# Scores by pairs of heads, with the last product of wide tiles in two 64-row halves

## The reference

```
q_nop = (c_Q @ Wq_up)          # 16 heads x 128
q_pe  = rope(c_Q @ Wq_pe)      # 16 heads x 64
k_nop, v = split(c_KV @ Wkv_up)  # 8 heads x 128 each, each used by two query heads
k_pe  = rope(rms_norm(x @ Wk_pe))  # 64, shared by all heads
scores = ([q_nop, q_pe] . [k_nop, k_pe]) * 192**-0.5, causal mask
y = softmax(scores) @ v
out = y @ Wo
```

## Time and profile before

| | us |
|---|---|
| median of 3 timed runs (lowest, highest) | 1826.86 (1822.85, 1830.7) |
| profiled execution, its own time | 1830.16 |
| its span, first to last instruction | 1828.4 |
| TensorE busy | 1724.3 (94%) |
| VectorE busy | 1293.5 (71%) |
| ScalarE busy | 1129.1 (62%) |
| GpSimd busy | 423.1 (23%) |
| mean granted TensorE clock (share of full) | 0.984 |

### The profile page before, as it was taken

How to read it: one execution, slowest core, us unless ns; L and a number is a source line. 1 busy time by engine, 2 the same in 40 slices (tenths; PEclk the granted TensorE clock), 3 DMA queues, 4 the chain that set the end, 5 groups by cost and what they waited for, 6 DMA issues and landing times.

```text
span 1828.4 us, 29329 instructions
## 1 busy us (share of the span) xinstructions
PE 1724.3 (94%) x9200; PEld 903.2 (49%) x9200; DVE 1293.5 (71%) x3368; ACT 1129.1 (62%) x2463; POOL 423.1 (23%) x1042
## 2 busy tenths in 40 slices
PE   4678999999999999999999999998999999999998
PEld 3344455544454545545554445554445444555443
DVE  5667677768677677776767777776767767777674
ACT  5566666657566566655656566665656656666563
POOL 1223222122221222222221222212222222221110
PEclk9799999999999999999999999999999999999999
DMA  9336788877868888785978867787876878877775
GB/s 257 82 63 113 129 138 156 153 134 139 144 115 158 149 145 147 144 150 92 161 127 158 154 124 139 146 149 129 146 143 127 152 138 147 150 144 145 144 147 104
DMA packets 911733, 255.05 MB, mean 139 GB/s; under 512 B 897368, under 2 KB 899674, under 8 KB 911194
## 3 DMA queue, kind: packets, MB, share of 16 engines
q1 hardware_dynamic: 902336, 235.29, 72.9%
q10 hardware_dynamic: 8794, 15.80, 2.8%
q0 software_dynamic: 448, 2.10, 0.5%
HBM read 20.32 MB, written 8.39 MB: 16 GB/s over the span
## 4 chain that ended last, share of the span: by engine, by line
PE 63%; issue 12%; DVE 10%; DMA 8%; ACT 3%; POOL 3%; SPq 1%; DVEq 0%; ACTq 0%; POOLq 0%
DMA FT<-F 6%; PE bank L539 5%; PE bank L543 5%; PE bank L542 5%; PE bank L540 5%; PE bank L541 5%; PE bank L563 5%; PE bank L564 4%; PE bank L565 4%; PE bank L580 4%; PE bank L582 4%; PE bank L581 4%; DVE F L1244 2%; DVE P L1230 2%; DMA Q<-QS 1%
## 5 line engine op out<-in xcount | busy, mean ns | idle before, releaser
L838 ACT ACTIVATE P<-P,nm 128x512 f32<-128x512 f32 (+7 forms) x512 | 395.5, 772 | 614.7 <-DVE nm L1230 613.6
L1230 DVE CUSTOM_DVE_ANT_0 P<-bank,mask,neg 128x512 f32<-128x512 f32 (+7 forms) x512 | 416.5, 814 | 330.9 <-PE bank L543 326.5
L1244 DVE SCALAR_TENSOR_TENSOR F<-P,rc,F 128x512 f16<-128x512 f32 (+7 forms) x512 | 420.1, 821 | 4.5 <-ACT F L833 3.8
L833 ACT ACTIVATE F<-P,rc 128x512 f16<-128x512 f32 (+7 forms) x512 | 389.7, 761 | 19.0 <-DVE rc L1238 12.7
L1417 POOL TENSOR_SCALAR sn<-sm 128x1 f32<-128x1 f32 x512 | 140.6, 275 | 578.0 <-ACT P L838 575.3
L539 PE MATMUL bank<-K,Q 128*128 128x512 f16 (+3 forms) x768 | 251.3, 327 | 5.4 <-DMA Q<-QS 5.1
L563 PE MATMUL bank<-FT,V 128*128 128x512 f16 x576 | 220.3, 382 | 34.9 <-DMA FT<-F 33.0
L541 PE MATMUL bank<-K,Q 128*128 128x512 f16 (+3 forms) x768 | 251.3, 327 | 0.0
L542 PE MATMUL bank<-K,Q 128*128 128x512 f16 (+3 forms) x768 | 251.3, 327 | 0.0
L540 PE MATMUL bank<-K,Q 128*128 128x512 f16 (+3 forms) x768 | 251.3, 327 | 0.0
L543 PE MATMUL bank<-K,Q 128*128 128x512 f16 (+3 forms) x768 | 251.2, 327 | 0.0
(11 more groups left out here) (191 smaller groups left out, 2596.6 us busy)
## 6 DMA issues: line engine op xcount, KB each, us to landing
out<-X ACTq DMA_DIRECT2D x32, 256.0 KB, 3.7
X<-in_x ACTq DMA_DIRECT2D x28, 256.0 KB, 3.1
FT<-F SPq DMA_TRANSPOSE x352, 4.2
wo<-in_Wo SPq DMA_DIRECT2D x4, 1024.0 KB, 9.3
V<-CC SPq DMA_DIRECT2D x32, 64.0 KB, 2.0
Q<-QS SPq DMA_TRANSPOSE x128, 4.1
X<-in_x SPq DMA_DIRECT2D x4, 256.0 KB, 7.5
ua<-in_Wq_up SPq DMA_DIRECT2D x1, 1024.0 KB, 9.3
```

The source lines that it names most:

```text
L833: return e.eng.activation(dst, src, ACT.Copy, scale=scale)
L838: e.eng.activation(m.P[:, u % 4, 0:w], m.P[:, u % 4, 0:w], ACT.Exp, bias=m.nm[:, u % 8:u % 8 + 1], scale=-1.0, accum_out=m.sm[:, u % 8:u % ...
L1230: e.eng.tensor_tensor_reduce(out=m.P[:, u % 4, 0:w], in0=m.pS[u % 2][:, off:off + w], in1=m.mask[:, 1024 - w:1024], scale=m.neg[:, :], sca ...
L1244: e.eng.scalar_tensor_tensor(out=m.F[:, slot, at + w:at + 2 * w], in0=m.P[:, u % 4, 0:w], scalar=m.rc[:, u % 8:u % 8 + 1], in1=m.F[:, slot ...
```

## The change

TensorE's score goes by pairs of heads (`pair(n, p)`, heads 2p and 2p+1), at quarters 0 and 2. In tiles with i >= 4 (`halved`) the first four products of both heads come first; then the last product is done with 64 rows for each head: for the even head rows 0 to 63 of block 8+h and of BLO, for the odd head rows 64 to 127, into the two heads' different banks, cut by cut. For this the rotated query parts lie as high, low, low, high in a pair of heads (`rotated_parts`), so that both heads' high part is where its half reads it; the product of low with low is no longer made in these tiles. `combine` is done in two halves, after quarters 1 and 3. The lists of VectorE, ScalarE, GpSimd and SyncE go by pairs too: two maxima one after the other, two exponents, both scaled parts, two transposes.

```diff
+def halved(i):
+    return i >= 4
...
+def rotated_parts(m, n):
+    return m.QS[:, n % 2, 1024:1536].rearrange("p (h a d) -> p h a d", h=2, a=4)
...
+    def pair(n, p):
...
+        for h in (2 * p, 2 * p + 1):
+            u = 4 * n + h
+            e.wait_ge(s.mk, u - 1)
+            for lo, hi in cuts:
+                o, keys = m.pS[u % 2][:, off + lo:off + hi], slice(base + lo, base + hi)
+                e.eng.matmul(o, Q[:, h, :], K[:, AHI, keys], start=True, stop=False)
+                e.eng.matmul(o, Q[:, h, :], K[:, ALO, keys], start=False, stop=False)
+                e.eng.matmul(o, Q[:, 4 + h, :], K[:, AHI, keys], start=False, stop=False)
+                e.eng.matmul(o, Q[:, 8 + h, :], K[:, BHI, keys], start=False, stop=False)
+                if not halved(i):
+                    op = e.eng.matmul(o, Q[:, 8 + h, :], K[:, BLO, keys], start=False, stop=True)
+            if not halved(i):
+                op.then_inc(s.s, 1)
+        if halved(i):
+            for lo, hi in cuts:
+                for h, top in ((2 * p, 0), (2 * p + 1, 64)):
+                    o, keys = m.pS[h % 2][:, off + lo:off + hi], slice(base + lo, base + hi)
+                    op = e.eng.matmul(o, Q[top:top + 64, 8 + h, :], K[top:top + 64, BLO, keys], start=False, stop=True)
+                    if hi == cuts[-1][1]:
+                        op.then_inc(s.s, 1)
...
-            if n + AHEAD < N:
-                score(n + AHEAD, q)
+            if q % 2 == 0 and n + AHEAD < N:
+                pair(n + AHEAD, q // 2)
...
-            if q == 3 and n:
-                combine(n - 1)
-    combine(N - 1)
+            if q % 2 and n:
+                combine(n - 1, q // 2)
+    combine(N - 1, 0)
+    combine(N - 1, 1)
```

VectorE's list of a block, after the change (ScalarE's, GpSimd's and SyncE's are changed alike):

```diff
+        wide = n + AHEAD < N and halved(where(n + AHEAD)[1])
+        for p in range(2):
+            u = 4 * (n + AHEAD) + 2 * p
+            if p == 0 and t and g == 1:
+                accumulate(t - 1)
+            if p == 0 and n and wide:
+                values_lo(n - 1)
             if u < 4 * N:
                 maximum(u)
+                maximum(u + 1)
+            if p == 0 and n and not wide:
+                values_lo(n - 1)
...
             if u <= 4 * N:
                 scaled_lo(u - 2)
+            if p == 0 and n + 2 * AHEAD < N:
+                queries.rotate(n + 2 * AHEAD)
+            if u <= 4 * N:
+                scaled_lo(u - 1)
+            if u < 4 * N:
+                inverse(u)
+                inverse(u + 1)
+            if p and n + 2 * AHEAD < N:
                 queries.queries_lo(n + 2 * AHEAD)
...
+            if t + LEAD < T and (g, p) == (2, 0):
+                tiles.x_signs(t + LEAD)
```

More of the change, by code:

```diff
@@ L544, in score @@
         op.then_inc(s.s, 1)
+    def pair(n, p):
+        b, i, g = where(n)
+        off, cuts = score_cuts(i)
+        base = key_slot(b, 0) * 128
+        Q, K = m.Q[:, n % 2, :, :], m.K
+        e.wait_ge(s.q_in[n % 2], 16 * (n // 2 + 1))
+        e.wait_ge(s.k_in, 16 * (n // NG + 1))
+        for h in (2 * p, 2 * p + 1):
[18 more added lines that the diff above has]
+                        op.then_inc(s.s, 1)
     def weigh(n, j):
@@ L565, in weigh, with combine @@
         e.eng.matmul(o, V[:, 1, :], hi, start=False, stop=(j == i)).then_inc(s.pv, 1)
-    def combine(n):
+    def combine(n, p):
         b, i, g = where(n)
         e.wait_ge(s.yl, n + 1)
-        if g == 0:
+        if g == 0 and p == 0:
             e.wait_ge(s.wol, 16)
@@ L576, in combine @@
         W = m.WO[:, g, :, :]
-        for h in range(4):
+        for h in (2 * p, 2 * p + 1):
             yh, yl = m.YH[:, n % 2, h * 128:h * 128 + 128], m.YL[:, n % 2, h * 128:h * 128 + 128]
@@ L888, in scalar_attention @@
         t, g = divmod(n, NG)
-        for q in range(4):
-            u = 4 * (n + AHEAD) + q
-            if q == 0 and n:
+        for p in range(2):
+            u = 4 * (n + AHEAD) + 2 * p
+            if p == 0 and n:
                 values_hi(n - 1)
-            if q == 3 and n + 2 * AHEAD < N:
-                queries.queries_hi(n + 2 * AHEAD)
             if u < 4 * N:
                 exponent(u)
-            if u <= 4 * N:
-                scaled_hi(u - 1)
-            if q == 2 and n + 2 * AHEAD < N:
+                exponent(u + 1)
+            if p and n + 2 * AHEAD < N:
                 queries.rotated_hi(n + 2 * AHEAD)
[L901 to L916, removed]
+                queries.queries_hi(n + 2 * AHEAD)
+            if t and t + LEAD - 1 < T and (g, p) == (0, 0):
+                tiles.squares(t + LEAD - 1)
+                tiles.rms_root(t + LEAD - 1)
+            elif t and t + LEAD - 1 < T and (g, p) == (0, 1):
+                tiles.parts_hi(t + LEAD - 1)
+            elif t + LEAD < T and (g, p) == (1, 0):
+                tiles.ln_root(t + LEAD)
+            elif t + LEAD < T and (g, p) == (1, 1):
+                tiles.norm(t + LEAD)
+                tiles.x_hi(t + LEAD)
+            elif t + LEAD < T and (g, p) == (3, 1):
+                tiles.down_out(t + LEAD, m.pY[(n + 1) % 2])
+            if u < 4 * N:
+                scaled_hi(u)
+                scaled_hi(u + 1)
+            if (g, p) == (2, 1) and t:
                 store_out(t - 1)
-            if (g, q) == (3, 3) and t + LEAD + 1 < T:
+            if (g, p) == (3, 1) and t + LEAD + 1 < T:
                 load_x(t + LEAD + 1)
@@ L1289, in vector_attention @@
         t, g = divmod(n, NG)
[L1290 to L1293, removed]
+        wide = n + AHEAD < N and halved(where(n + AHEAD)[1])
+        for p in range(2):
+            u = 4 * (n + AHEAD) + 2 * p
+            if p == 0 and t and g == 1:
+                accumulate(t - 1)
+            if p == 0 and n and wide:
+                values_lo(n - 1)
             if u < 4 * N:
                 maximum(u)
-            if u <= 4 * N:
[L1297 to L1303, removed]
-                scaled_lo(u - 2)
-            if q == 3 and n + 2 * AHEAD < N:
-                queries.queries_lo(n + 2 * AHEAD)
[L1307 to L1320, removed]
@@ new lines, in vector_attention @@
+                maximum(u + 1)
+            if p == 0 and n and not wide:
+                values_lo(n - 1)
+            if t and t + LEAD - 1 < T and (g, p) == (0, 1):
+                tiles.ffn_out(t + LEAD - 1, m.pY[(n + 1) % 2])
+            if u <= 4 * N:
+                scaled_lo(u - 2)
+            if p == 0 and n + 2 * AHEAD < N:
+                queries.rotate(n + 2 * AHEAD)
+            if u <= 4 * N:
+                scaled_lo(u - 1)
+            if u < 4 * N:
+                inverse(u)
+                inverse(u + 1)
@@ new lines, in vector_attention @@
+            if p and n + 2 * AHEAD < N:
+                queries.queries_lo(n + 2 * AHEAD)
+            if t and t + LEAD - 1 < T and (g, p) == (0, 0):
+                tiles.rms(t + LEAD - 1)
+            if t and t + LEAD - 1 < T and (g, p) == (0, 1):
+                tiles.parts_lo(t + LEAD - 1)
+            if t + LEAD < T and (g, p) == (0, 1):
+                tiles.stats(t + LEAD)
+            if t + LEAD < T and (g, p) == (1, 0):
+                tiles.ln(t + LEAD)
+            if t + LEAD < T and (g, p) == (2, 0):
+                tiles.x_signs(t + LEAD)
@@ L1418, in scale_sum @@
                             ALU.mult).then_inc(s.sm, 1)
-    for u in range(4 * AHEAD - 1):
+    for u in range(4 * AHEAD):
         scale_sum(u)
@@ L1425, in gpsimd_attention @@
         t, g = divmod(n, NG)
[L1426 to L1429, removed]
+        for p in range(2):
+            u = 4 * (n + AHEAD) + 2 * p
+            if u < 4 * N:
+                scale_sum(u)
+                scale_sum(u + 1)
             if n + 2 * AHEAD < N:
-                if q == 1:
+                if p == 0:
                     queries.rotated(n + 2 * AHEAD)
-                elif q == 2:
+                else:
                     queries.rotated_lo(n + 2 * AHEAD)
-            if (g, q) == (1, 3) and t + LEAD < T:
-                tiles.x_lo(t + LEAD)
[L1437 to L1441, removed]
+            if t and t + LEAD - 1 < T:
+                if (g, p) == (1, 0):
+                    tiles.rotate_keys(t + LEAD - 1)
+                elif (g, p) == (1, 1):
+                    tiles.keys(t + LEAD - 1)
+            if (g, p) == (1, 1) and t + LEAD < T:
+                tiles.x_lo(t + LEAD)
 class SyncTiles:
@@ L1562, in sync_attention @@
         t, g = divmod(n, NG)
-        for q in range(4):
-            u = 4 * (n + AHEAD) + q
-            if u <= 4 * N + 1:
+        for p in range(2):
+            u = 4 * (n + AHEAD) + 2 * p
+            if p == 0 and n + AHEAD + 1 < N:
+                turn_queries(n + AHEAD + 1)
+            if u <= 4 * N:
                 turn_probabilities(u - 2)
-            if q == 0 and n + AHEAD + 1 < N:
-                turn_queries(n + AHEAD + 1)
-            if (g, q) == (2, 1) and t + LEAD < T:
+                turn_probabilities(u - 1)
+            if (g, p) == (2, 0) and t + LEAD < T:
```

(2 more changed lines are left out.)

14 lines of the change are left out of this document (9 added, 5 removed).

## The result

The changed kernel takes 1780.5 us by the median (1777.9 to 1784.0), the kernel before 1828.8 beside it: ratio 0.974, interval 0.970 to 0.978, so 48 us or 2.6% faster. The forecast was 1804, its own range 1790 to 1815. The profiled execution took 1778.6 us.

What follows compares the result with a forecast made beforehand. TensorE was taken to be limited by columns. From the profiled 1830.2 us, -45.0 (columns), +25.1 (change-overs), +3.5 (second half) and -8 (order) give 1805.8; less 3.3, rounded up for clock: 1804 us, own range 1790 to 1815, with rivals 1777 to 1844.

Steps and rivals of the forecast that it cites:

- Columns removed: Score's fifth product, tiles i >= 4: two 64-row halves side by side save one pass per pair, 128 pairs, -45.0 us.
- Change-over: TensorE switching between whole array and halves, 256 times: one weight load not hidden, 98 ns each, +25.1 us.
- Rival A: TensorE's change-over is free or nearly so, as weight loads are now: 1777 us, chance 0.12.
- Rivals B and C: Each change-over: B drains without exposed load, 193 ns, 1827 us, chance 0.13; C tail then load, 261 ns, 1844, 0.12.
- Second half's start: 64-row halves on TensorE are issued one after the other: 0 to 7.0 us, half taken, +3.5 us.
- The order by pairs: Reordered lists by pairs of heads, combination in halves: -8 us in sum, ends -34 and +21.
- (1): TensorE's `queries.up` in short tiles: half a combination ahead hides some 10 of 15.4 us waiting for the rotation, -10.
- (2): values_lo stands behind both maxima in tiles not wide, so TensorE waits before the half combination: 0 to +9, taken +6.
- (3): Eight 2.9 us FT stalls, two a batch: x_signs behind scaled_lo makes the transfer 1.5 us earlier, -12 us.
- (4): TensorE's clock: the sum was only rounded up to 1804 for the clock that a new wait would cost.
- (5): Short tile weighed while a wide one is scored, 0 to +12, taken +4; FT transfers issued together queue, +4.
- Rival E: Pair order makes TensorE wait for maxima or FT in short tiles, plus lower clock, +26: 1830 us, chance 0.10.

Runs made afterwards that it cites:

- same-half experiment: Changed kernel with the odd head's 64-row product also on rows 0 to 63, so both use the same half of the array: 1822.8 us, ratio 0.997.
- the order alone: Changed kernel with halved() false for every tile: lists by pairs and combination in halves, but the fifth product 128 rows for each head: 1795.2 us, ratio 0.982.
- the one-piece kernel: Changed kernel with the combination in one piece again, after the fourth quarter: 1759.9 us, ratio 0.962.
- with the old lists: Kernel before with only TensorE's scores by pairs and halves for i >= 4; combination in one piece, other engines' lists by quarters: 1874.4 us, ratio 1.025.
- the early reciprocals: Changed kernel with both reciprocals directly behind both maxima on VectorE, ahead of values_lo, scaled_lo and the rotation: 1907.2 us, ratio 1.043.
- the late first pair: Changed kernel with the first quarter's weigh products ahead of the first pair of scores: 1835.7 us, ratio 1.003.

## Why the prediction was right and wrong

- **Columns removed**, -45.0: measured -45.5. Right, and shown by the same-half experiment to come from the halves side by side.
- **Change-over**, 98 ns each, +25.1: measured 96 and 92 ns, +24.1. Right in size, and in part by luck: I took it for the length of one load (98 ns), but the product starts 0.01 behind its load. What is exposed is the load's start, 0.09 us after the old kind's columns are through. Rival A (free) gave 1777, close to the result, and is still refuted: the result came near it by another term. Rivals B and C, tail and all, are refuted.
- **Second half's start**, +3.5: 3 ns a cut, under 1 us in all.
- **The order by pairs**, -8: measured -32.5. This is the step that failed; its bound of -34 held it. Term by term, from before to the order alone: (1) `queries.up`, -10: its waits went from 15.4 to 0.6, but not because of the half combination, as the one-piece kernel has them at 4.6. They are 4.9 us or less in every kernel with pairs on TensorE and stayed (14.4) where only the reciprocal was moved. (2) values_lo, +6: the wait is the one I named, but it measured 16.0 there and 19.1 in the changed kernel, and taking the half combination out gave back 20.6. I had counted VectorE's list, but not that values_hi stands on ScalarE behind a scaled_hi that waits for the reciprocal; with values_lo ahead of the maxima everywhere, 12.6 of the 19.1 stayed. (3) FT, -12 with x_signs as the reason: the waits fell by 24 us, and x_signs is worth 2 of them. What I left out is, by these runs, that a pair puts one more head's score ahead of the first weigh product, and, as it seems the smaller part, VectorE's second longest wait, 96.9 us for the sum. I had read VectorE's wait for TensorE (326.5) and concluded that it is early; an engine that waits there can still be late in the short tiles. (4) The clock: I put its return with the stalls at nothing; by the starts some 10 us came back with them (8.6 in the changed kernel). (5) Short beside wide, +4, and queueing, +4: no row of after shows either; they were not tried by themselves. With (1) to (4) the waits changed by -14.8, +16.0 and -24, the clock by some -10: -33, against the 32.5 measured.
- **Rival E** (new waits for maxima in the pair order) is what happens with the old lists, 93.9 us, and not with the new ones (0.3 us). VectorE's busy time, which I held unchanged at 1293 us, is 1318.8 (74%, not 72%), for the same number of operations; the cause is open.
- The Trainium skill, "TensorEngine Tiling (Array Packing)", section Key Properties, has it that a change of mode drains TensorE and that tiles run in parallel. The traces fit both, at 92 to 103 ns a change and 3 ns between the halves, though they show only that the load starts late, not what it waits for. The 53 ns that I estimated from the drain in the Trainium skill, "TensorE: Matmul & The Clock Gate", section Step-by-step: what each phase is for, is too little; the measurement decides.

What stays open: how the 32.5 us divide between the reciprocal's place and the pair's. In the old lists the first is worth 12.7. In the new ones neither was put back as it had been: the early reciprocals (+127) stand where no sum can be ready, and the late first pair (+55) leaves no score ahead of the first weigh product, where the kernel before had one.

## What to carry to other kernels

Two 64-row products in different halves of the array cost one pass, and going there and back costs about 190 ns here. By that price, as an estimate (190 ns at 2.4 GHz), it pays from about 450 columns saved in one visit, and so only if the products of one kind stand together: with a visit for each cut it lost. When lists are reordered for one engine, read the waits of all the others first: here two lines moved in VectorE's list, a small operation that waited for a chain over three engines, brought 12.7 us by themselves. And try each part of a reorder alone; one part of this one cost 20 us.

## What the runs showed of the hardware that was not expected

GpSimd's sum of the rotated parts (same line, same shape) took 728 ns before by the mean and 1197 after, its scale 275 and 468. Before, VectorE's operation beside it was mostly the maximum, which reads a PSUM bank and the mask; after, it is scaled_lo, which reads P and F in SBUF.

```profile
L1370 POOL TENSOR_TENSOR R<-R,R 128x256 f32<-128x256 f32 x128 | 93.2, 728 | 224.4 <-DVE R L1037 224.4
...
L1416 POOL TENSOR_TENSOR R<-R,R 128x256 f32<-128x256 f32 x128 | 153.3, 1197 | 92.3 <-DVE R L1078 92.3
```

One pair of rows of the kernel after, VectorE's and GpSimd's:

```profile
370.92 1.01 DVE L1285 SCALAR_TENSOR_TENSOR F<-P,rc,F 128x768 f16<-128x768 f32 x1
371.09 1.43 POOL L1416 TENSOR_TENSOR R<-R,R 128x256 f32<-128x256 f32 x1 [0.75 <-DVE R L1078]
```

When GpSimd starts, 0.84 us of scaled_lo are left (370.92 + 1.01 - 371.09), and its 1.43 us are these plus 0.59. So it is in all 117 records of the kernel after in which scaled_lo was running when this sum began: its length is what was left of scaled_lo plus 0.58 to 0.59 us, so the sum gets nowhere until scaled_lo has ended. In the other 11 it takes 0.72 to 0.73, and so it does in the kernel before in all 128 (0.72 to 0.74), where scaled_lo never ran at its start, though in 69 of them it started during it. The scale takes about 0.21 us beside anything else, and beside a running scaled_lo what is left of that plus 0.07 by the median. Only pairs of operations as they fell are compared here; no run changes this alone. No wait of TensorE names GpSimd, and VectorE waits 3.9 us for its sums, so it cost no time that TensorE shows.
